# Masked graph attention on 8192 rows: the denominators of the whole-row visits one pair later, the last two pairs row tile by row tile, and rows of 260 words for the rounded h

## What is computed

```
h  = max(layernorm(x), 0)                       # x: 8192 x 256
h1 = h @ a[:256];  h2 = h @ a[256:]
e  = leaky_relu(h1 + h2.T, 0.01)                # 8192 x 8192
attention = softmax(where(adj > 0, e, -9e15), axis=1)
out = x + attention @ h
```

## Time and profile before

| | |
|---|---|
| median of three runs | 1642.61 us |
| the profiled execution | 1641.76 us, span 1640.0 us |
| TensorE busy | 98% of the span |
| VectorE busy | 87% |
| ScalarE busy | 72% |
| GpSimd busy | 24% |
| product matmuls | 3 x 4096, one started about every 0.12 us |

### The profile page before, as it was taken

One profiled execution on the slowest core, in us unless ns is written; L12 is line 12 of the kernel. 1 busy time (PEld: TensorE's weight loads), 2 busy tenths in 40 slices (PEclk: granted clock), 3 DMA queues, 4 the chain that ended last, 5 costly groups with the idle time before them and its releaser, 6 DMA issues.

```text
span 1640.0 us, 38962 instructions
## 1 busy us (share of the span) xinstructions
PE 1600.4 (98%) x13350; PEld 1589.2 (97%) x13350; DVE 1431.7 (87%) x2008; ACT 1182.1 (72%) x1240; POOL 397.8 (24%) x487
## 2 busy tenths in 40 slices
PE   5999999999999999999999999999999999999998
PEld 4999999999999999999999999999999999999998
DVE  7899999999999988888788888888888888888887
ACT  7788778777778766767767767767767766767763
POOL 6344224453344311201201201201301300300400
PEclk9999999999999999999999999999999999999999
DMA  6666767877777777657666656666756756666662
GB/s 206 217 204 217 229 209 223 245 221 245 244 225 232 232 210 229 198 169 206 198 185 194 210 166 191 209 182 176 227 175 184 212 178 189 206 184 183 207 182 74
DMA packets 170376, 330.97 MB, mean 202 GB/s; under 512 B 8640, under 2 KB 26048, under 8 KB 170304
## 3 DMA queue, kind: packets, MB, share of 16 engines
q1 hardware_dynamic: 145248, 288.90, 58.2%
q10 hardware_dynamic: 25056, 41.13, 7.7%
HBM read 308.90 MB, written 21.10 MB: 201 GB/s over the span
## 4 chain that ended last, share of the span: by engine, by line
PE 79%; issue 4%; ACT 4%; POOL 4%; DVE 3%; DMA 2%; ACTq 0%; DVEq 0%; POOLq 0%
PE acc L869 25%; PE acc L872 24%; PE acc L871 24%; PE T L831 6%; POOL stage L381 2%; DMA xo<-part_sums 2%; ACT mask L500 1%; POOL xb L390 1%; DVE W L710 1%; POOL xb L392 1%; ACT hb L564 1%; ACT w_hi L509 1%; ACT stage L563 1%; DVE w_lo L720 1%; ACT stage L528 0%
## 5 line engine op out<-in xcount | busy, mean ns | idle before, releaser
L869 PE MATMUL acc<-h_hi,w_hi 128*128 128x258 f32 (+1 forms) x4096 | 1183.3, 289 | 17.9 <-DVE w_lo L720 14.0
L872 PE MATMUL acc<-h_hi,w_lo 128*128 128x258 f32 (+1 forms) x4096 | 1154.8, 282 | 0.0
L871 PE MATMUL acc<-h_lo,w_hi 128*128 128x256 f32 (+1 forms) x4096 | 1149.4, 281 | 0.0
L509 ACT ACTIVATE w_hi<-W 128x1024 fp32r<-128x1024 f32 x512 | 538.4, 1057 | 359.9 <-DVE W L710 301.1
L869 PEld LDWEIGHTS acc<-h_hi,w_hi 128*128 128x128 f32 x4096 | 772.2, 189 | 24.7 <-ACT w_hi L509 14.4
L710 DVE SCALAR_TENSOR_TENSOR W<-r_rep,g_all,T 128x512 f32<-128x512 f32 (+1 forms) x1024 | 718.4, 743 | 68.7 <-DVE w_lo L720 41.3
L871 PEld LDWEIGHTS acc<-h_lo,w_hi 128*128 128x128 f32 x4096 | 777.3, 190 | 0.0
L872 PEld LDWEIGHTS acc<-h_hi,w_lo 128*128 128x128 f32 x4096 | 773.0, 189 | 0.0
L720 DVE SCALAR_TENSOR_TENSOR w_lo<-W,w_hi 128x1024 fp32r<-128x1024 f32 x512 | 651.7, 1273 | 100.6 <-PE acc L872 71.4
L500 ACT ACTIVATE mask<-adj_in,mhalf 128x2048 fp8e5<-128x2048 int32 x256 | 509.5, 1990 | 26.9 <-POOL xb L392 26.6
L390 POOL TENSOR_TENSOR xb<-xb,stage 128x256 f32<-128x256 f32 x60 | 55.8, 930 | 697.3 <-ACT hb L564 697.3
(11 more groups left out here) (68 smaller groups left out, 221.9 us busy)
## 6 DMA issues: line engine op xcount, KB each, us to landing
adj_in<-in_adj_dram SPq DMA_DIRECT2D x256, 1024.0 KB, 5.4
part_sums<-stage ACTq DMA_DIRECT2D x24, 516.0 KB, 6.5
xo<-part_sums ACTq DMA_DIRECT2D x24, 516.0 KB, 3.6
r_rep<-r_rows SPq DMA_DIRECT2D x39, 256.0 KB, 3.6
xb<-in_x_dram ACTq DMA_DIRECT2D x15, 512.0 KB, 3.9
out_dram<-xb ACTq DMA_DIRECT2D x15, 512.0 KB, 3.2
xb<-in_x_dram SPq DMA_DIRECT2D x14, 512.0 KB, 6.1
xo<-in_x_dram SPq DMA_DIRECT2D x2, 512.0 KB, 5.3
```

Source lines behind the costliest of these rows:

```text
L509: nc.scalar.activation(w_hi[:, k % HL, :], W[:, k % 2, :], ACT.Relu).then_inc(s_hi, 1)
L869: nc.tensor.matmul(acc[:, t, 0:WC], w_hi[:, k % HL, cols], rhs_hi, start=start and u == 0, stop=False)
L871: nc.tensor.matmul(acc[:, t, 0:D], w_hi[:, k % HL, cols], rhs_lo, start=False, stop=False)
L872: last = nc.tensor.matmul(acc[:, t, 0:WC], w_lo[:, k % LL, cols], rhs_hi, start=False, stop=stop and u == 1)
```

## The change

**One.** In rest visits `denominators` runs at k = 4 and not at k = 3, `normalise` at k = 4 to 7 and not at k = 3 to 6, and `store_out` in the visit's last group of four pairs (side work 8, pair 28 of 32) and not at k = 7. Full visits stay.

VectorE's stream in the first rest visit, before: w_lo<-W,w_hi is `subtract`, W<-r_rep,g_all,T is `weights`, and the four rows between are `denominators`.

```
-        h_hi = sb("h_hi", [P, NT, WC], f32r)
+        h_hi = sb("h_hi", [P, NT, HW], f32r)
...
+        one = sb("one", [P, 1], f32)
+        ones = one[:, 0:1].to_broadcast([P, P])
...
-                if V.prev in ("full", "rest"):
-                    if k == 2:
-                        load_x_again(V)
+                if V.prev in ("full", "rest") and k == 2:
+                    load_x_again(V)
+                if V.prev == "full":
                     if 3 <= k < 3 + G:
                         normalise(V.f, k - 3)
                     if k == 7:
+                        store_out(V)
+                if V.prev == "rest":
+                    if 4 <= k < 4 + G:
+                        normalise(V.f, k - 4)
+                    if k == 2 * PI:
                         store_out(V)
...
+                    if last and V.prev == "rest":
+                        side_work(V, 2 * PI + k)
...
-                if V.prev in ("full", "rest") and k == 3:
+                if (V.prev, k) in (("full", 3), ("rest", 4)):
                     denominators(V)
...
+                nc.vector.tensor_scalar(zrow[:, col], d_hi, d_lo, 0.0, ALU.add, ALU.is_equal).then_inc(s_tail, 1)
+                nc.vector.tensor_scalar(den[:, col], d_hi, d_lo, TINY, ALU.add, ALU.max).then_inc(s_tail, 1)
                 dve.wait_ge(s_tail, TAIL * t + 1)
...
+                dve.wait_ge(s_tail, TAIL * t + 2)
+                nc.vector.reciprocal(rinv[:, col], den[:, col]).then_inc(s_tail, 1)
                 dve.wait_ge(s_tail, TAIL * t + 4)
...
+            def last_products(c, g, k):
+
+                pe.wait_ge(s_hi, g + 1)
+                pe.wait_ge(s_lo, g + 1)
+                for t in range(2):
+                    row_tile(c, k, t, False, False)
+                pe.wait_ge(s_hi, g + 2)
+                pe.wait_ge(s_lo, g + 2)
+                for t in range(2):
+                    row_tile(c, k + 1, t, False, True).then_inc(s_acc, 1)
+                row_tile(c, k, 2, False, False)
+                row_tile(c, k + 1, 2, False, True).then_inc(s_acc, 1)
+                row_tile(c, k, 3, False, False).then_inc(s_used, 1)
+                row_tile(c, k + 1, 3, False, True).then_inc(s_used, 1)
```

More of the change, by code:

```diff
@@ L846, in sum_h @@
                 for e in range(G):
-                    last = nc.tensor.matmul(hs_acc, ones[:], h[:, e, :], start=c == 0 and e == 0,
+                    last = nc.tensor.matmul(hs_acc, ones, h[:, e, :], start=c == 0 and e == 0,
                                             stop=False, skip_group_check=True)
@@ L853, in add_row_sums, with row_tile @@
                 pe.wait_ge(s_hs, G * (NB - Q) + 1)
-                nc.tensor.matmul(hs_acc, ones[:], hsum[:], start=False, stop=True,
+                nc.tensor.matmul(hs_acc, ones, hsum[:], start=False, stop=True,
                                  skip_group_check=True).then_inc(s_hm, 1)
+            def row_tile(c, k, t, start, stop):
+                for u in range(2):
+                    tile = G * c + 2 * (k % 2) + u
+                    cols = slice(u * BLK + t * P, u * BLK + (t + 1) * P)
+                    rhs_hi = h_hi[:, ds(tile, 1), 0:WC].rearrange("p o w -> p (o w)")
+                    rhs_lo = h_lo[:, ds(tile, 1), :].rearrange("p o w -> p (o w)")
+                    nc.tensor.matmul(acc[:, t, 0:WC], w_hi[:, k % HL, cols], rhs_hi,
+                                     start=start and u == 0, stop=False)
+                    nc.tensor.matmul(acc[:, t, 0:D], w_hi[:, k % HL, cols], rhs_lo, start=False, stop=False)
+                    last = nc.tensor.matmul(acc[:, t, 0:WC], w_lo[:, k % LL, cols], rhs_hi,
+                                            start=False, stop=stop and u == 1)
+                return last
             def products(V, c, g, k, start, stop):
@@ L863, in products @@
                         pe.wait_ge(s_free, G * (V.v - 1) + t + 1)
[L864 to L873, removed]
+                    last = row_tile(c, k, t, start, stop)
                     if stop and t < G - 1:
@@ L886, in steps @@
                     kc = k // 2
-                    m = c + kc
+                    m = c + kc if V.head else None
                     if V.head and m == 0 and k == 0:
@@ L891, in steps @@
                         pe.wait_ge(s_hl, m + 1)
+                    if V.tail and last and kc == 1:
+                        if k == 2:
+                            last_products(c + kc, n * PI + k, k)
+                        continue
                     products(V, c + kc, n * PI + k, k, first and k == 0, last and k == PI - 1)
```

23 lines of the change are left out of this document (8 added, 15 removed).

## The result

The changed kernel takes 1619.14 us (four runs, 1618.86 to 1619.58), the kernel before 1642.74 us (1642.26 to 1643.20) in the same comparison. The ratio is 0.9861, with a 95% interval of 0.9849 to 0.9872. The forecast was 1620.0 us with a range of 1614.0 to 1627.0. The profiled execution took 1619.30 us with a span of 1617.5 us, 22.5 us less than the span before. By the medians the gain is 23.6 us; where the difference comes from is told under "The start".

The account below looks back on a forecast made before the run. TensorE, busy 98% of the span, was taken to bound the kernel. Gains of 16.9 + 2.7 + 3 = 22.6 us took the profiled 1641.76 to 1619.2; with 0.85 for the runs' median, 1620.0 us (range 1614.0 to 1627.0).

Parts of the forecast that it names:

- part three: Rows of h_hi padded to 260 words, so odd tiles start aligned for TensorE's product matmuls: 3 us less.
- The bound and the size of part one: TensorE bounds the kernel; rest-visit stalls total 17.7 us, of which moving denominators to k = 4 wins 16.9.
- VectorE's wait for the add at k = 4: Rest visits: GpSimd's add blocked by a `subtract`, leaving VectorE 0.6 to 0.7 us of its wait.
- ScalarE's late mask: Rest visits, `convert` behind the fourth `normalise`: 0.1 us margin, 0.8 us allowed; as rival 0.9 us late each, 1627 us, 12%.
- The store costs nothing at pair 28: Rest visits' store moved 20 pairs later: one issue on ScalarE where no other side work stands, costing nothing.
- Part two: Program end: reordered last two pairs let VectorE start earlier, at 1.27 us per row tile for 1.62: 2.7 us less.
- bounds of +9.8 and -3: Pitch of h_hi's rows: most gain if 1.2 ns goes from 2 x 4096 matmuls; loss if new tile addresses cost.
- the upper bound: Matmuls reading h_hi: the pitch gains 9.8 us, from medians of 283 and 281 ns; as rival 1613 us, 12%.
- The Trainium skill's 16-byte lines: Rows of h_hi touch 65 lines at either start, so the pitch gives nothing; as rival 1623 us, 22%.
- The fourth rival: Every product matmul: moved tiles make TensorE's reads collide, slower than before, 1652 us at 2.4 ns each; chance 3%.
- The total: Whole kernel: rest-visit stalls, program end and row pitch together win 22.6 us, giving 1620.0 us.

Follow-up runs that it names:

- e6: Kernel before with the new order of the last two pairs and the old six operations per row tile: 1643.99 us in a single run.
- e10: Changed kernel with the fourth normalise of a rest visit moved to pair 28 and its store to pair 31: 1618.43 us, ratio to the kernel before 0.9855.
- e3: Kernel before with rows of h_hi 260 words apart, the ones as one column and the four small tiles in one: 1638.93 us, ratio 0.9979.
- e8: Kernel before with h_hi's rows still of 258 words but all starting 8 bytes later: 1639.27 us, ratio 0.9982.
- e1: Kernel before with only the rest-visit moves of denominators, normalise and store_out: 1625.92 us, ratio 0.9899.
- e7: Kernel before with the new five operations per row tile and the old order of the last two pairs: 1641.53 us in a single run.
- e4: Kernel before with h_hi rows kept at 258 words and a 512-byte gap behind h_hi that moves the other tiles: 1642.49 us, ratio 1.0002.

## Why the store had to move too (e5)

e5 is the changed kernel with the store at the old place:

```
-                    if k == 2 * PI:
+                    if k == 7:
                         store_out(V)
...
-                    if last and V.prev == "rest":
-                        side_work(V, 2 * PI + k)
```

> The changed kernel with the store of a rest visit's block issued at k = 7, right behind the last normalise, as before the change. Theory: ScalarE waits there for the last finish and issues a DMA, which puts the next convert about 2.5 us later (from 796.1 to 798.6 us in the visit that starts at 778.5), so TensorE's transpose behind the seventh pair waits 2.6 us in place of 0.12 in each of the eight rest visits: rest windows of 27.2 us and 1639 us in all. Rival (the mask is wanted later than that; the store was moved for nothing): 24.8 us and 1619.2 us.

Measured: 1646.28 us, ratio 1.0031 (1.0017 to 1.0044), so slower than before the change. The stall is the one laid out, and there is more. ScalarE in a rest visit, the store and the mask behind it:

```profile
801.06 0.40 ACTq L570 DMA_DIRECT2D out_dram<-xb  x1
801.82 2.00 ACT L501 ACTIVATE mask<-adj_in,mhalf 128x2048 fp8e5<-128x2048 int32 x1 [2.61 <-POOL xb L393]
```

TensorE there:

```profile
803.96 1.11 PE L835 MATMUL T<-ident,mask 128*128 128x128 f32 x4 [2.63 <-ACT mask L501]
804.72 0.56 PE L868 MATMUL acc<-h_hi,w_hi 128*128 128x258 f32 x1
805.08 0.41 PE L870 MATMUL acc<-h_lo,w_hi 128*128 128x256 f32 x1
...
806.76 0.28 PE L868 MATMUL acc<-h_hi,w_hi 128*128 128x258 f32 x1
```

And windows around it, with the granted clock third from the end:

```profile
799.90:803.20 3.30, 1.42 (x12) 1.22 (x11) 1.41 (x2) 1.38 (x1) 1.05 (x2) 1.00 0.37 126
803.20:806.70 3.50, 2.74 (x13) 2.75 (x14) 1.66 (x2) 3.50 (x4) 0.00 (x0) 0.51 0.50 109
806.70:810.00 3.30, 3.30 (x30) 3.30 (x30) 2.12 (x3) 1.97 (x2) 0.00 (x0) 1.00 0.95 284
```

In the changed kernel the same mask of the visit that starts at 776.85:

```profile
796.12 1.99 ACT L501 ACTIVATE mask<-adj_in,mhalf 128x2048 fp8e5<-128x2048 int32 x1
```

```profile
798.05 0.28 PE L873 MATMUL acc<-h_hi,w_lo 128*128 128x258 f32 x1
798.24 0.65 PE L837 MATMUL T<-ident,mask 128*128 128x128 f32 x4
```

There it starts 19.27 us into its visit with no wait, and TensorE goes from the last product to the transpose in 0.19 us. Here the visit starts at 779.85, and the mask comes 21.97 us into it, right behind the store's issue, for which ScalarE waited 2.61 us on GpSimd's last operation on xb. TensorE then stands 2.63 us for the mask. Behind it the matmuls start 0.21 us apart and not 0.12, at the lower of the two clock levels (1.2 GHz), for 3.4 us. In this trace that followed in three of the eight rest visits and cost some 1.3 us each time; the windows of the other five were 2.8 us longer than full ones. 8 x 2.8 + 3 x 1.3 = 26.3 us, and the rest visits sum to 223.3 us where full ones sum to 196.8. The forecast of 1639 us had the stall and not the clock. The runs reach from 1643.5 to 1656.3 us, and their granted clocks go with it: the mean over the span is 0.997 in the fastest, 0.995 in those of 1646.5 to 1647.6 us and 0.989 in the slowest. By these figures the fastest spent some 10 us at the lower level and the slowest some 36 (an estimate: 0.011 x 1654.5 us of span / 0.5). That is more than eight stretches of 3.4 us, so in the slowest run one stretch for each rest visit isn't the whole of it; only the one execution has a trace.

## The start

The changed kernel is 1.6 us later than the one before at the end of its first eight pairs, which no step of the prediction explains. 0.25 us of it are there before the first product (20.43 and 20.18 us; all executions lie between 19.8 and 21.3). Two executions more, without an edit:

> The changed kernel once more, for its first 60 us. Theory: TensorE's half clock of 3.4 us near 21 us is chance, so another execution may have none, or two; the first 32 pairs take between 115.6 and 118 us and all behind them is the same to 0.1 us. Rival: it belongs to the changed kernel and is there again.

> The kernel before once more, for its first 60 us. Theory: its half clock at the start is chance too and may be there this time (its profiled execution had none), with 1.3 us more for the first eight pairs. Rival: it never has one there.

The window of the first eight pairs, in the first profile of the kernel before, and then in this second one:

```profile
20.18:56.72 36.54, 31.78 (x237) 29.52 (x237) 31.35 (x78) 30.10 (x48) 21.53 (x37) 1.00 0.59 187
```

```profile
20.95:58.52 37.57, 33.06 (x236) 31.00 (x237) 31.31 (x78) 30.21 (x48) 21.47 (x37) 0.95 0.59 182
```

Once at full clock, once with 0.95, and 1.0 us more for it. TensorE still waits for other engines at this point (before its first product at 20 us it had been idle most of the time), and gets its full clock or not from one execution to the next: the same program had it in one profile and not in the other, which takes the rival out for the kernel before. The changed kernel takes 37.86 us at 0.95 in both its profiles (and e6 38.86 us at 0.92). But e10, with the same start, had the full clock and took 37.05 us, and e3 had it too and took 37.04. So the clock is worth 0.8 us of the changed kernel's 1.3, and 0.5 us (37.05 less 36.54) stay at full clock.

These 0.5 us are a cost of part three. To make h_lo, GpSimd subtracts h_hi's rows from the full ones, four operations for four tiles, and TensorE waits for it here. Before, and in the changed kernel:

```profile
26.31 2.63 POOL L370 TENSOR_TENSOR h_lo<-hq,h_hi 128x256 fp32r<-128x256 f32 x4 [0.35 <-ACT h_hi L480]
...
36.17 3.61 POOL L370 TENSOR_TENSOR h_lo<-hq,h_hi 128x256 fp32r<-128x256 f32 x4 [0.62 <-ACT h_hi L480]
```

```profile
26.56 2.84 POOL L371 TENSOR_TENSOR h_lo<-hq,h_hi 128x256 fp32r<-128x256 f32 x4 [0.37 <-ACT h_hi L481]
...
37.48 3.81 POOL L371 TENSOR_TENSOR h_lo<-hq,h_hi 128x256 fp32r<-128x256 f32 x4 [0.63 <-ACT h_hi L481]
```

That is 0.2 us more for four tiles. One by one, and without the three or so of 1.6 to 1.8 us in each trace, such an operation of the first 60 us takes 0.73 to 0.75 us on an even tile and 0.64 to 0.66 on an odd one in the kernel before, 0.73 to 0.75 on both in the changed one, and in e8 the odd ones are the longer. So for GpSimd a row that starts at a multiple of 16 is the slow one, the other way round than for TensorE, and 260 words take its fast tiles away. In all five profiles with rows of 260 words the fourth and the sixth pair take 0.2 and 0.1 us longer than in the eight with 258, whatever the clock, and at full clock the second takes 0.2 us longer; these are the 0.5. Later TensorE doesn't wait for this.

So of the 1.6 us, 0.25 and 0.8 go with the execution and 0.5 with part three. The sum without what goes with the execution is 17.0 + 2.7 + 4.35 - 0.5 = 23.55, and by the medians the gain is 23.6 us.

## The fourth normalise at pair 28 (e10)

What is left in a rest visit is a mask 0.1 us late. e10 takes the fourth normalise out of the tight place:

```
-                    if 4 <= k < 4 + G:
+                    if 4 <= k < 3 + G:
                         normalise(V.f, k - 4)
                     if k == 2 * PI:
+                        normalise(V.f, G - 1)
+                    if k == 3 * PI - 1:
                         store_out(V)
```

> The changed kernel with the fourth normalise of a rest visit moved to pair 28 and its store to pair 31. Theory: the mask for the transpose behind the seventh pair is no longer 0.12 us late, so rest windows of eight pairs take 24.62 us in place of 24.75; 0.9 us less, 1618.3 us, which a comparison of runs can hardly tell from none. Rival (the mask is late for another reason): windows stay at 24.75 us.

Measured: 1618.43 us, ratio to the kernel before 0.9855 (0.9840 to 0.9870). Its full and rest windows:

```profile
751.20:775.80 24.60, 24.60 (x210) 24.60 (x209) 22.45 (x28) 20.32 (x24) 8.10 (x8) 1.00 0.71 212
775.80:800.40 24.60, 24.60 (x211) 24.60 (x210) 21.83 (x28) 19.98 (x20) 9.97 (x10) 1.00 0.69 218
```

The rest visit has no stall left, and the table's 196.80 us equals the full one's. The 0.9 us are shown by one trace; the runs alone (1617.37 to 1619.98) could not tell them from the changed kernel's.

## The prediction, step by step

**The bound and the size of part one:** right. 17.7 us of stalls were read from the windows and 17.9 were there (the full window was read 0.03 us too long); 0.8 us were to stay and 0.9 did.

**VectorE's wait for the add at k = 4:** the step that failed. It was to be 0.6 to 0.7 us in each visit, with an add of 4.5 us. In seven of eight visits the add took 3.5 to 3.6 us and VectorE did not wait. The last visit came out as forecast. GpSimd and VectorE in the visit at 776.85:

```profile
777.52 3.57 POOL L382 TENSOR_TENSOR stage<-stage,xo 128x258 f32<-128x258 f32 x4 [7.03 <-ACT stage L529]
```

```profile
780.41 1.76 DVE L728 SCALAR_TENSOR_TENSOR w_lo<-W,w_hi 128x1024 fp32r<-128x1024 f32 x1 [0.54 <-ACT w_hi L510]
782.09 0.15 DVE L740 TENSOR_TENSOR fin<-stage 128x4 f32<-128x4 f32 x1
```

and in the last one:

```profile
1516.38 4.56 POOL L382 TENSOR_TENSOR stage<-stage,xo 128x258 f32<-128x258 f32 x4 [7.10 <-ACT stage L529]
```

```profile
1519.11 1.23 DVE L728 SCALAR_TENSOR_TENSOR w_lo<-W,w_hi 128x1024 fp32r<-128x1024 f32 x1 [0.44 <-ACT w_hi L510]
1520.97 0.17 DVE L740 TENSOR_TENSOR fin<-stage 128x4 f32<-128x4 f32 x1 [0.64 <-POOL stage L382]
```

I had `subtract` start while the third add ran and then win against the fourth. It starts 2.9 us behind the first add and not 2.8, since it waits for ScalarE's `round_w` first (which I left out), and there it meets the start of the fourth add. In seven visits `subtract` takes 1.76 to 1.84 us in place of 1.23 and the add is not held up; in the last the fourth add takes 1.82 us in place of 0.75. Some 0.5 us fall on VectorE either way. That one of the two holds the other up for a whole operation agrees with the Trainium skill (SBUF — State Buffer, "shared port pair"); which of them does can't be had from a walk of this kind: the two starts lie within 0.01 us of each other in the first and in the last visit, with opposite outcomes, and in the last visit of e1 `subtract` starts 0.03 us ahead and is still the one that takes 1.85 us. It cost the forecast nothing: the denominators start 5.24 us into the visit (782.09 - 776.85), where 784.5 - 779.13 = 5.37 were forecast.

**ScalarE's late mask:** right, in part by luck. The walk put the `convert` 19.27 us into the visit (798.4 - 779.13), and there it was. From it a margin of 0.1 us was worked out, and 0.1 us in each visit allowed for all the same; measured is a lateness of 0.1 us in seven visits of eight, 0.92 us in all. The walk had left out the 0.13 us between the mask's end (796.12 + 1.99) and the transpose (798.24), a delay that it had counted for VectorE's w_lo (0.14). e5 and e10 show from both sides that this `convert` is what TensorE waits for.

**The store costs nothing at pair 28:** right; no wait of ScalarE is left there. What I had as a side remark, that its move makes the rest possible, is worth 26 us by e5, and the prediction had neither a price nor a rival for it.

**Part two:** right, 2.7 us forecast and measured; tiles of 1.25 us and not 1.27. e6 and e7 give its halves.

**Part three:** the mechanism was right, and the term was mis-sized: 3 us taken, 4.35 measured in the trace of the changed kernel, less 0.5 us that it costs at the start, and 3.4 us (2.0 to 4.9 by the interval of the ratio) between the runs of e3. That 3 lies near is luck, since it was a choice between bounds of +9.8 and -3. The row behind the upper bound hardly moved: medians of 283 and 281 ns before, 282 and 280 in the changed kernel, so those 2 ns are no measure of what the pitch wins. The gain is in the steps of odd tiles alone. The full window was to be 0.05 us shorter than before and is 0.09 (24.59 for 24.68). The Trainium skill's 16-byte lines (SBUF — State Buffer, "cachelines"), counted as lines touched, gave nothing for this part, and the measurement decides against that count. The fourth rival, colliding addresses, is out for this move by e4.

**The total:** 16.9 + 2.7 + 3 = 22.6 against 17.0 + 2.7 + 4.35, and from the spans 1.6 us less for the start, which I had not considered. That the spans differ by 22.5 us is luck: 1.35 us too little for part three and 1.6 us for the start all but cancel. By the medians the forecast is 1.0 us short of 23.6.

## What to carry to other kernels

When a helper engine's wait stalls the engine that bounds a kernel, take a window with the wait and one without: their difference is the most that moving the wait can win in that window, and here it was right to 0.2 us. Then walk the in-order streams of all engines behind the moved work, stores and their waits included: the same move with the store left in place would have made this kernel slower. Where a matmul's operand has rows that are not a multiple of 16 bytes apart, try a padded pitch; it was worth 0.2% here. Look also at the other engines that read the same rows: here GpSimd became slower by it.

## What the runs showed of the hardware

- A row of a matmul's moving operand (258 words of fp32) that starts 8 bytes past a multiple of 16 made three matmuls 2 to 4 ns slower (358 to 360 ns for 356); with rows 259 words apart starts at 4 and 8 took 358.8 ns and those at 12 took 355.4.
- GpSimd's fp32 subtraction of 128 x 256 that reads such a row took 0.73 to 0.75 us where the row starts at a multiple of 16 bytes and 0.64 to 0.66 us where it starts 8 bytes past one (even and odd tiles of the kernel before; the other way round in e8).
- With TensorE idle for 1.3 to 1.4 us, eight times in the kernel before, no lower clock followed; with 2.5 to 2.6 us, eight times in e5, 3.4 us at the lower level followed three times.
- The same program gets the full clock in its first 40 us in one execution and not in another, for 1.0 us of difference over the first eight pairs (the kernel before, two profiles).
- GpSimd's fp32 tensor operation and VectorE's `subtract` with two SBUF inputs hold each other up: where they met, one took its usual time and the other 1.76 to 1.84 us for 1.23 (`subtract`, seven rest visits) or 1.82 for 0.75 (the fourth add of the last rest visit). The one with the earlier start was not always the one that went first.
